# Uniform order of stages in all turns, and the first four tiles' norms, inverses, adds and routing two tiles at a time

## The reference

```
k = layernorm(x);  v = ctx
for each channel, over the 64 steps of a sequence, with decay w and bonus u (a scan, kept stable by a running maximum):
    y = (p + exp(u + k) * v) / (q + exp(u + k))
    p = exp(w) * p + exp(k) * v;   q = exp(w) * q + exp(k)
x = x + y
h = layernorm(x)
probs = softmax(h @ gate_w)                      # 32 experts
w, sel = top_k(probs, 8);  w = w / sum(w)
each expert takes its first C = 2 * (1024 * 8 / 32) = 512 tokens, in order
x = x + sum over chosen experts of w * (silu(h @ w_gate[e]) * (h @ w_up[e])) @ w_down[e]     # 96 inner units
```

## Time and profile before

| | us |
|---|---|
| median of 3 runs | 273.46 |
| lowest, highest | 271.75, 275.55 |
| profiled execution, its own time | 274.06 |
| its span, first to last instruction | 272.3 |
| TensorE busy in the span | 246.9 (91%) |
| mean granted TensorE clock | 0.979 |

### The profile page before, as it was taken

One profiled execution on the slowest core, in us unless ns is written; L12 is line 12 of the kernel. 1 busy time (PEld: TensorE's weight loads), 2 busy tenths in 40 slices (PEclk: granted clock), 3 DMA queues, 4 the chain that ended last, 5 costly groups with the idle time before them and its releaser, 6 DMA issues.

```text
span 272.3 us, 4017 instructions
## 1 busy us (share of the span) xinstructions
PE 246.9 (91%) x1077; PEld 190.6 (70%) x1077; DVE 134.8 (49%) x334; ACT 133.4 (49%) x239; POOL 161.3 (59%) x140
## 2 busy tenths in 40 slices
PE   6529997299997999899999999999999999999993
PEld 1414484187876887687878787878778787878772
DVE  5598956217853685458725344234424333334233
ACT  2981430853536935595458454525344353534420
POOL 5161200724776679657876784868685867768620
PEclk9999999858999999999999999999999999999998
DMA  6945100000505042512341324141415050700002
GB/s 201 266 144 143 41 2 0 1 1 12 169 15 159 16 118 74 137 36 62 111 118 58 99 76 131 46 120 54 133 40 140 33 156 17 225 28 0 0 2 78
DMA packets 43359, 22.24 MB, mean 82 GB/s; under 512 B 34128, under 2 KB 43344, under 8 KB 43344
## 3 DMA queue, kind: packets, MB, share of 16 engines
q1 hardware_dynamic: 42496, 21.63, 27.6%
q10 hardware_dynamic: 848, 0.43, 0.5%
...
## 4 chain that ended last, share of the span: by engine, by line
PE 62%; issue 13%; DVE 11%; POOL 5%; ACT 4%; DMA 2%; ACTq 1%; POOLq 0%; DVEq 0%
PE bank L686 37%; PE bank L704 7%; PE bank L708 7%; PE bank L705 6%; POOL wlo L342 3%; PE bank L603 2%; DMA bonus_sb<-in_L_xattn_u_dram 2%; PE bank L643 1%; DVE bank L900 1%; DVE t_sb L1037 1%; DVE state L888 1%; PE bank L693 1%; DVE t_sb L1031 1%; DVE state L890 1%; POOL rstd L355 1%
## 5 line engine op out<-in xcount | busy, mean ns | idle before, releaser
L374 POOL TENSOR_TENSOR t_lo<-t_sb,t_hi 128x512 fp32r<-128x512 f32 x47 | 60.8, 1294 | 59.5 <-ACT t_hi L533 57.6
L342 POOL TENSOR_TENSOR wlo<-raw,whi 128x768 fp32r<-128x768 f32 x48 | 88.5, 1845 | 7.9 <-ACT whi L502 7.7
L686 PE MATMUL bank<-h_hi,whi 128*128 128x512 f32 x192 | 80.9, 421 | 0.0
L1031 DVE TENSOR_TENSOR t_sb<-bank,s_sb 128x512 f32<-128x512 f32 x48 | 33.2, 692 | 91.7 <-ACT s_sb L528 59.5
L686 PE MATMUL bank<-h_lo,whi 128*128 128x512 f32 x192 | 76.5, 399 | 0.0
L686 PE MATMUL bank<-h_hi,wlo 128*128 128x512 f32 x192 | 76.5, 398 | 0.0
L533 ACT ACTIVATE t_hi<-t_sb 128x512 fp32r<-128x512 f32 x48 | 30.3, 632 | 86.2 <-DVE t_sb L1037 86.2
L502 ACT ACTIVATE whi<-raw 128x768 fp32r<-128x768 f32 x48 | 39.9, 836 | 9.3 <-PE bank L708 8.1
L686 PEld LDWEIGHTS bank<-h_hi,wlo 128*128 128x128 f32 x192 | 36.5, 190 | 8.8
L686 PEld LDWEIGHTS bank<-h_hi,whi 128*128 128x128 f32 x192 | 36.9, 192 | 7.7
L686 PEld LDWEIGHTS bank<-h_lo,whi 128*128 128x128 f32 x192 | 36.7, 191 | 7.7
...
## 6 DMA issues: line engine op xcount, KB each, us to landing
...
```

Source lines behind the costliest of these rows:

```text
L342: pool.tensor_tensor(split_view(wlo, slot, part), raw_parts(slot, part), split_view(whi, slot, part).bitcast(F32), ALU.subtract).then_inc( ...
L374: pool.tensor_tensor(t_lo[k % 2][:], t_sb[:], t_hi[k % 2][:].bitcast(F32), ALU.subtract).then_inc(t_lo_ready, 1)
L686: last = nc.tensor.matmul(ps[:], up_weight(w, slot, part, k, j), h[:, k, tokens], start=(i == 0), stop=(i == len(terms) - 1))
L1031: nc.vector.tensor_tensor(t1_sb[:], w_ps[:], s_sb[:], ALU.mult).then_inc(t1_ready, 1)
```

## The change

Every turn of the first half now has one order, the first too, with `early` as its plain `back`. The additional buffers let both norms of a tile be under way together (slot 3 for the second norm of a slot-2 unit), and the guards in `power` and `norm_stats` go. VectorE adds the back in step 0 ahead of the front's statistics and does `h_low` and `largest` in step 2, `choose` and `begin_sums` in 3, `end_sums` in 4, `mix` and `weigh` in 5. GpSimd does both powers in step 0. ScalarE copies the route of the tile before in step 0, norms back and front in step 1, takes h in 2, does all exps in 3. TensorE does `turn_h` and `turn_kv` in step 1 behind the projection of step 2, logits in 2, ranks at the end of 3, `turn_mixed` in 5 behind the next projection. In the last turn without a front `weigh` and `turn_parts` go a step earlier.

In the introduction the first four tiles are added, normed, and routed as two units; the two halves' logits and parts get banks 0 and 4; their counts are made by one sum of four matmuls (`first_counts`). ScalarE interleaves norms, exps and inverses of the units, the fifth tile's inverse is by Ln and Exp as well, VectorE does unit 0's recurrence ahead of the fifth tile's statistics, and `mix(early)` behind the routing. The fillers go from 18 to 12, and two groups of 5 go.

The diff, cut to its core (blank lines left out):

```diff
+    def norm_slot(self, norm):
+        return 3 if self.slot == 2 and norm is self.second_norm else self.slot
...
-        logits_ps = [bank[4][:, 0:HT * E], bank[7][:, 256:256 + E]]
-        ranks_ps = [bank[7][:, 0:(HT + 1) * E], bank[7][:, 288:288 + 2 * E]]
-        parts_ps = [bank[4][:, 256:512].bitcast(BF16), bank[7][:, 384:384 + P // 2].bitcast(BF16)]
+        logits_ps = [bank[0][:, 0:NT * E], bank[4][:, 0:NT * E], bank[7][:, 256:256 + E]]
+        first_counts_ps = bank[7][:, 0:E]
+        ranks_ps = bank[7][:, 288:288 + 2 * E]
+        parts_ps = [*(bank[i][:, 256:256 + NT * P // 2].bitcast(BF16) for i in (0, 4)),
+                    bank[7][:, 384:384 + P // 2].bitcast(BF16)]
...
-        early = Unit(2, HT, 1, 2, (2, 5), True)
-        first_routed = Unit(0, 0, HT, 0, None, False)
-        early_routed = Unit(1, HT, 1, 1, None, True)
+        early = Unit(2, HT, 1, 2, (2, 5), True, by_log=True)
+        first_routed = [Unit(n, NT * n, NT, n, None, False) for n in range(2)]
+        early_routed = Unit(2, HT, 1, 2, None, True)
...
@@ -346,14 +353,9 @@
             def power(u, norm):
                 pool.wait_ge(var_ready, norm + 1)
-                if u.slot == 2 and u is not early:
-                    if norm is u.first_norm:
-                        pool.wait_ge(h_normed, u.n)
-                    else:
-                        pool.wait_ge(k_normed, u.n + 1)
-                chain.link(pool.tensor_tensor(rstd[u.slot][:], var[u.slot][:], neg_half[:, 0:u.tiles], ALU.pow))
-                pool.tensor_tensor(offset[u.slot][:], neg_mean[u.slot][:], rstd[u.slot][:], ALU.mult).then_inc(rstd_ready, 1)
...
@@ -377,20 +378,21 @@
                 for k in range(TURN_STEPS):
                     if not final or k < TURN_STEPS - 1:
                         product_low(it * TURN_STEPS + (half * STEPS + k), k)
+                    if back and k == 0:
+                        power(back, back.second_norm)
                     if front and k == 0:
                         power(front, front.first_norm)
-                    if front and k == 5:
-                        power(front, front.second_norm)
                     ahead = k // GT + 1
                     if ahead == 1 or not final:
                         split_low(ahead % 2, k % GT, it * 2 + (half * GROUPS + ahead))
-                    if back and k == 0:
+                    if back and k == 2:
                         keep_low(back)
...
+            turn(0, 0, later(3), early)
...
             nc.scalar.preload_act_table_set("natural_log_exp_and_others")
-            decay_factors()
-            for u in first_units:
-                norm_x(u)
-            for u in first_units:
-                exps(u)
+            norm_x(first_units[0])
+            decay_factors(NT, factors[0])
+            bonus_gain()
+            exps(first_units[0])
+            norm_x(first_units[1])
+            exps(first_units[1])
             norm_x(early)
+            decay_factors(1, factors[1])
             act.wait_ge(gate_landed, 16)
             nc.scalar.activation(gate_hi[:], gate_sb[:], ACT.Copy).then_inc(gate_hi_ready, 1)
-            for part in range(3):
+            invert(first_units[0])
+            exps(early)
+            for part in range(2):
                 split_high(0, part, 0)
-            exps(early)
-            invert()
+            invert(first_units[1])
+            split_high(0, 2, 0)
             spread_experts()
             for u in first_units:
                 norm_h(u)
             for u in first_units:
                 take_h(u)
-            route_exps(first_routed)
+            invert(early)
+            for u in first_routed:
+                route_exps(u)
...
-            def turn(half, it, front, back, routed, first_turn=False, final=False):
+            def turn(half, it, front, back, routed, before=None, first_turn=False, final=False):
+                def first_step():
+                    if first_turn:
+                        for u in first_routed:
+                            take_route(u)
+                    elif before:
+                        take_route(before)
+                def norms():
+                    norm_h(back)
+                    if front:
+                        norm_x(front)
                 def all_exps():
                     if front:
                         exps(front)
-                    if back:
-                        route_exps(routed)
+                    route_exps(routed)
                     fetch_silu(it * 2)
-                beside = {1: lambda: take_h(back), 2: all_exps}
-                if first_turn:
-                    beside[0] = lambda: (take_route(first_routed), norm_h(early))
+                beside = {0: first_step, 1: norms, 2: lambda: take_h(back), 3: all_exps}
+                if not front:
+                    beside[5] = lambda: take_route(routed)
                 if half == 0 and not first_turn:
                     fetch_silu(it * 2 - 1)
                 for k in range(TURN_STEPS):
@@ -551,12 +570,6 @@
                     ahead = k // GT + 1
                     if ahead == 1 or not final:
                         split_high(ahead % 2, k % GT, it * 2 + (half * GROUPS + ahead))
-                    if front and k == (1 if first_turn else 0):
-                        norm_x(front)
-                    if front and k == TURN_STEPS - 1:
-                        norm_h(front)
-                    if back and k == TURN_STEPS - 1:
-                        take_route(routed)
...
@@ -617,9 +630,11 @@
                 pe.wait_ge(h_normed, u.n + 1)
                 if u.slot == 2:
-                    pe.wait_ge(route_ready, u.n - 1)
+                    pe.wait_ge(route_ready, u.n)
+                    if u is early:
+                        pe.wait_ge(counted, 1)
...
@@ -627,13 +642,12 @@
             def logits(u):
-                if u is first_routed:
+                if u is first_routed[0]:
...
@@ -644,21 +658,20 @@
                                                 start=(n == 0), stop=(n == len(terms) - 1))
                 last.then_inc(logits_ready, 1)
+            def first_counts():
+                pe.wait_ge(mask_ready, 2)
+                pe.wait_ge(consts_ready, 2)
+                chosen = [mask[slot][:, t, :] for slot in range(2) for t in range(NT)]
+                for n, m in enumerate(chosen):
+                    last = nc.tensor.matmul(first_counts_ps, ones_bf[:], m, start=(n == 0), stop=(n == len(chosen) - 1))
+                last.then_inc(ranks_ready, 1)
...
@@ -739,28 +752,16 @@
                     slot, j = k // GT, k % GT
                     if half or not first_turn or k:
                         project(n, half, 1, slot, j, it * 2 + (half * GROUPS + slot))
-                    if back and first_turn and k == 1:
-                        project(n + 1, half, 0, 0, 2, 0)
-                        turn_h(back)
                     if first_turn and k == 0:
-                        pe.wait_ge(route_ready, ROUTED if half else 1)
+                        pe.wait_ge(route_ready, ROUTED if half else 2)
                         if half == 0:
                             pe.wait_ge(tables_ready, 1)
                     if j == 0:
...
-                    if front and k == 1:
-                        turn_kv(front)
-                    if back and k == 3:
-                        ranks(routed)
-                    if front and k == 5:
-                        turn_mixed(front)
                     if half == 0 and first_turn and k == 0:
-                        keep_clock(5)
-                    elif half == 0 and first_turn and k == 1:
                         pass
                     elif k < TURN_STEPS - 1 or not last_turn:
                         project(n + 1, half, 0, (k + 1) // GT % 2, (k + 1) % GT,
...
+                    if back and k == 1:
+                        turn_h(back)
+                    if front and k == 1:
+                        turn_kv(front)
+                    if back and k == 2:
+                        logits(routed)
+                    if front and k == 5:
+                        turn_mixed(front)
                     if k > 0:
...
-                    if back and k == 0 and not first_turn:
-                        turn_h(back)
-                    if back and k == 1:
-                        logits(routed)
-                    if back and k == 5:
+                    if back and k == 3:
+                        ranks(routed)
+                    if back and k == (5 if front else 4):
                         turn_parts(routed)
...
-            keep_clock(18)
+            keep_clock(12)
             turn_h(first_units[0])
             turn_h(first_units[1])
-            keep_clock(5)
-            logits(first_routed)
+            logits(first_routed[0])
+            logits(first_routed[1])
             project(0, 0, 0, 0, 0, 0)
             project(0, 0, 1, 0, 0, 0)
             project(1, 0, 0, 0, 1, 0)
-            ranks(first_routed)
```

(56 more changed lines are left out.)

149 lines of the change are left out of this document (66 added, 83 removed).

## The result

The changed kernel takes 269.31 us, median of four runs (268.98 to 270.35), against 273.53 (271.75 to 275.55); ratio 0.984, interval 0.980 to 0.988. Forecast were 264.3 and -9.2. The span went from 272.3 to 266.8, -5.5; what lies around it in the profiled execution grew from 1.76 to 2.33 (269.13 - 266.8), so that the profiled executions differ by 4.9 and the medians by 4.2. Of the 5.0 us between 264.3 and 269.31, 3.7 are span, 0.6 lie around it, and the rest is that I took the median 0.6 under the profiled execution, where it is 0.2 over it.

A forecast was written before the change was run, and what follows sets the result against it. TensorE, busy 246.9 of 272.3 us, was taken as the bound, with time to win only where it waits or runs slowly. Terms -1.8 -3.9 -4.0 +1.0 -0.55 -0.2 +0.25 gave -9.2, so 264.3 us; range 260.8 to 269.6.

The forecast's parts named there:

- The stand in the first turn: First turn, from the routing weights to the sixth tile's transposes: 10.06 us becomes 6.14, so 3.9 won.
- 4.0 won, or nothing: First turn behind the stand: the low clock costs 4.0 us, won if the clock stays up, otherwise nothing.
- If the waits are 1.9 and 0.5 with transposes between, it stays up: First turn: TensorE's shorter remaining waits keep the clock at 1.00, as waits in turns 1 and 2 did; worth 4.0 us.
- Rival A: The clock falls again in the first turn, giving back the 4.0: 268.3 us; chance 0.13.
- The introduction: Start to first routing weights: routing in two units and shorter norm chain bring the weights to 41.9, 1.8 us earlier.
- rival B: The clock comes up late in the introduction, with 12 fillers and thin logits; price 1.5 to 3, 266.5 us; chance 0.10.
- The new wait at a turn's end: TensorE waits for VectorE's mix ahead of turn_mixed in turns with a front: 1.0 us a turn, bounds 0 to 2.0.
- The wait at L603 goes: Turns 1 and 2: waits of 1.55 and 1.22 at the front's transposes vanish; with the new wait, -0.55 and -0.2.
- Turn 3: Turn without a front: the mask and turn_parts, now behind step 4, may cost 0.25 us.
- C: ScalarE's exps, moved to step 3, delay sums and mask by up to 4.0 a turn: 276.8 at worst; chance 0.04.
- D: GpSimd's power makes the first turn's norm late again; only the introduction is won: 272 us; chance 0.05.

The follow-up runs named there:

- a3: Changed kernel with the sixth tile's first norm on ScalarE put back behind step 1 in the first turn alone; 271.88 us, ratio 0.992.
- b1: Kernel before, with 19 matmuls of zeros added to the down sums in the first turn's 4.62 us stand; 270.95 us, ratio 0.988.
- b2: Kernel before, with two fillers ahead of each of the four tiles' logits in the introduction; 274.02 us, ratio 1.001.
- after: The changed kernel itself, without further edits; 269.31 us, ratio 0.984 to the kernel before.
- a2: Changed kernel with two fillers ahead of the first unit's logits and four between the two units' logits in the introduction; 267.93 us, ratio 0.980.
- a5: Changed kernel with the 18 fillers of the kernel before in place of 12 in the introduction; 268.81 us, ratio 0.981.
- e1: Changed kernel with 16 fillers in the introduction, from between the two units' transposes to behind the logits; 266.93 us, ratio 0.973.
- a4: Changed kernel, TensorE's order alone: turn_mixed behind down in step 5, routing parts' transposes in the next turn's step 0; 272.06 us, ratio 0.992.
- a6: Changed kernel with the fifth tile's inverse by VectorE's reciprocal again instead of ScalarE's Ln and Exp; 271.55 us, ratio 0.990.
- d1: Changed kernel with turn_mixed and turn_parts later, ScalarE's route copy in step 1, turn 3's parts transposed in step 5; 265.36 us, ratio 0.970.
- a1: Changed kernel with eight matmuls of zeros added to the down sums in the first turn's remaining stand; 267.98 us, ratio 0.979.
- a7: Changed kernel with TensorE's transposes of the front (turn_kv) behind down in step 1 instead of ahead of it; 265.87 us, ratio 0.971.

## Why the prediction was wrong

- **The stand in the first turn** (-3.9): right, -3.88, by the same links; a3 shows the norm's place on ScalarE to be worth 1.3 of it. The 4.0 us that the low clock cost the profiled execution of the kernel before were right as well (b1: 4.0), but they were that launch's; b2 lost 1.3 at the same place, and the ratio of b1 says 3.3. "4.0 won, or nothing" left out what lies between.
- **"If the waits are 1.9 and 0.5 with transposes between, it stays up"**: this step failed. The waits were 1.74 and 0.33, and the clock fell in four of the seven profiles that had this stand unfilled (after, a2, a5, e1; not a4, a6, d1). I had set turn 1's wait of 1.55 beside it; but that was one wait with four transposes behind it, and here 3.1 us hold two waits and six transposes. That the difference lies there, and not in the launch, is not shown. Rival A had it at 0.13 and priced it at the whole 4.0; it gave back 1.5 (a1: 1.54; 1.33 by the medians), because the low clock lasted from 49.0 to 52.3 where TensorE had worked at it from 53.77 to some 62.7. With the new wait (below) the line came to -1.47 for -3.0.
- **The introduction** (-1.8): mis-sized, -1.15. VectorE's chain was put right (parts ready at 40.56, forecast 40.25). The last projection's matmuls ended at 41.55 instead of 39.5, because logits started 0.6 later and the clock was low from 35.6 to 39.0: this is rival B, which I had tied to the shortened fillers. a5 speaks against that, e1 for the stretch of stands, transposes and logits behind them. Without the low clock the weights come at 41.6 to 42.2 (a2, e1), so the forecast 41.9 was right to 0.3 once the clock is taken out; how much the change gains there over several launches is not shown, since the kernel before varies as well (43.71, 47.50).
- **The new wait at a turn's end** (+1.0): right in kind, and in size for turn 1 only. It is 0.61 ahead of turn_mixed in all three turns; behind turn_parts come 0.13, 0.41 and 0.06, so the sums are 0.74, 1.02 and 0.67. d1 takes out both and wins 1.25 and 0.88.
- **"The wait at L603 goes"** (-1.55 and -1.22): it left 0.54 a turn, since the front's norm came later than I had put it: in turn 1 it ended 7.89 behind the turn's first projection (71.30) and its transposes started at 8.13, where I had both at 7.45. And I read the old waits off the idle column and the new ones off sums of starts: on the same footing the old ones were 1.70 and 1.37. The new sums are 1.56 and 1.21, so the waits fell by 0.14 and 0.16, where 0.55 and 0.2 were forecast; the turns even grew by 0.18 and 0.17, and the 0.3 between is spread over starts of matmuls behind another kind, under 0.1 each, down's above all. a7 takes the 0.54 out.
- **Turn 3** (+0.25): mis-sized, +0.59; 0.37 is the wait for the parts in step 4 (d1: -0.34 when it moves).
- Rivals C and D did not come about: no wait for mix over 0.61, and the norms came in time. (C's price has a slip: 264.3 and 12 are 276.3, not 276.8.)

Summed, the misses are 0.65 + 1.5 + 0.7 + 0.4 + 0.3 + 0.1 = 3.7 of span. Another 0.6 lies around the span, and for that I have no cause; in the four launches of the changed kernel it is 1.75 to 2.78.
